# A two-layer kernel on one core: new order at both ends of the first attention, and SiLU from exponentials and logarithms

## The reference, cut to what matters

```python
x = x + xattn(norm(x), ctx)     # 16 heads; head h sees every 16th key, from h on: 128 keys for each
x = x + ssm(norm(x))            # below
x = x + swiglu(norm(x))         # weights of three levels, activations of 8 bits
x = x + gated(norm(x), ctx)
x = x + self_attention(norm(x)) # 16 heads, relative bias
x = x + mlp(norm(x))            # 8 bits

def ssm(x):
    xi, res = split(x @ W_in)                  # 256 channels each
    u = silu(conv4(xi) + conv_b)
    dt, B, C = split(u @ W_x)                  # 8, 16, 16
    delta = softplus(dt @ W_dt + b_dt)
    h = exp(delta * A) * h + delta * B * u     # step by step over 128 tokens, 16 states
    y = sum(h * C) + u * D
    return (y * silu(res)) @ W_out
```

## Time and profile before

| | us |
|---|---|
| median of 3 runs | 279.73 |
| lowest, highest | 277.42, 280.04 |
| span of the profiled execution | 278.8 |
| busy in it: PE, DVE, ACT, POOL | 209.7, 205.7, 151.6, 74.6 |

### The profile page before, as it was taken

How to read it: one execution, slowest core, us unless ns; L and a number is a source line. 1 busy time by engine, 2 the same in 40 slices (tenths; PEclk the granted TensorE clock), 3 DMA queues, 4 the chain that set the end, 5 groups by cost and what they waited for, 6 DMA issues and landing times.

```text
span 278.8 us, 4790 instructions
## 1 busy us (share of the span) xinstructions
PE 209.7 (75%) x1557; PEld 141.2 (51%) x1559; DVE 205.7 (74%) x585; ACT 151.6 (54%) x510; POOL 74.6 (27%) x73
## 2 busy tenths in 40 slices
PE   6896988898786977777762577999996699973313
PEld 4475877676752322222131354777785688851102
DVE  6358648873069999999957975767767499985675
ACT  4357659643685555555317773245336689853420
POOL 5013000049305777777794010000001000001000
PEclk9688999999979799999996899999999899997555
DMA  7999700068830000000000005000000000000001
GB/s 225 429 393 414 317 2 2 0 74 93 94 45 0 1 0 1 0 0 0 2 1 0 1 0 150 2 0 2 0 1 0 4 1 2 0 4 0 4 0 38
DMA packets 6745, 16.06 MB, mean 58 GB/s; under 512 B 320, under 2 KB 5056, under 8 KB 5696
## 3 DMA queue, kind: packets, MB, share of 16 engines
q1 hardware_dynamic: 6720, 15.75, 19.7%
HBM read 13.39 MB, written 2.35 MB: 56 GB/s over the span
## 4 chain that ended last, share of the span: by engine, by line
PE 38%; DVE 24%; POOL 13%; issue 12%; ACT 9%; DMA 2%; POOLq 0%; SPq 0%; another core or an unknown queue 0%; DVEq 0%; ACTq 0%
PE bank L1076 31%; POOL region L392 13%; ACT probs L477 3%; PE bank L1416 3%; DVE region L775 2%; DVE region L758 2%; DMA ctx_T_sb<-ctx_T 2%; PE bank L1189 2%; DVE neg_max L753 1%; DVE xn L685 1%; DVE stats L680 1%; PE bank L1093 1%; DVE ext L1040 1%; DVE ext L1041 1%; DVE v_heads L698 1%
## 5 line engine op out<-in xcount | busy, mean ns | idle before, releaser
L1076 PE MATMUL bank<-region,early_sb 128*128 128x512 f32 x64 | 36.8, 661 | 11.8 <-POOL region L392 11.6
L392 POOL TENSOR_TENSOR region<-region 128x512 f32<-128x512 f32 x32 | 40.5, 1268 | 14.5 <-DVE region L900 14.5
L900 DVE TENSOR_TENSOR_SCAN region<-region,bank 128x512 f32<-128x512 f32 x32 | 38.7, 1211 | 0.0
L1076 PE MATMUL bank<-k_groups,region 128*128 128x128 f32 x256 | 35.7, 285 | 1.2 <-ACT k_groups L459 1.2
L1076 PEld LDWEIGHTS bank<-k_groups,region 128*128 128x128 f32 x256 | 32.2, 198 | 3.2 <-ACT k_groups L459 1.8
L361 POOL TENSOR_TENSOR xb<-x,rows_sb 128x512 f32<-128x512 f32 x3 | 3.8, 1261 | 101.0 <-DVE x L790 43.2
L477 ACT ACTIVATE probs<-bank,neg_max 128x128 f32<-128x128 f32 x64 | 22.6, 367 | 12.9 <-DVE neg_max L753 12.5
L1076 PE MATMUL bank<-ctx_T_sb,region 128*32 128x128 f32 (+1 forms) x288 | 26.8, 345 | 3.4 <-DMA ctx_T_sb<-ctx_T 2.2
L477 ACT ACTIVATE probs<-region,neg_max 128x128 f32<-128x128 f32 x64 | 24.9, 390 | 5.7 <-DVE neg_max L758 5.5
L1076 PEld LDWEIGHTS bank<-region,early_sb 128*128 128x128 f32 x64 | 10.1, 195 | 33.2 <-POOL region L392 32.6
L775 DVE COPY region<-bank 128x512 f32<-128x512 f32 x32 | 21.8, 682 | 5.6 <-PE bank L1189 5.6
(11 more groups left out here) (198 smaller groups left out, 410.1 us busy)
## 6 DMA issues: line engine op xcount, KB each, us to landing
ctx_sb<-ctx SPq DMA_DIRECT2D x4, 1024.0 KB, 24.5
ctx_T_sb<-ctx_T SPq DMA_DIRECT2D x3, 1024.0 KB, 10.5
late_sb<-late SPq DMA_DIRECT2D x1, 2416.0 KB, 18.4
bias_scratch<-bias_vec SPq DMA_DIRECT2D x1, 2040.0 KB, 24.7
ctx_T_sb<-ctx_T SPq DMA_DIRECT2D x2, 512.0 KB, 6.2
region<-bias_scratch SPq DMA_DIRECT2D x1, 1024.0 KB, 5.7
early_sb<-early SPq DMA_DIRECT2D x1, 512.0 KB, 3.7
region<-taps SPq DMA_DIRECT2D x1, 512.0 KB, 18.9
```

Source lines behind the costliest of these rows:

```text
L392: done(pool.tensor_tensor(read[:, k % 3, :], state[:, k % 3, :], c_sb[:, n % 2, :], ALU.mult), "read")
L900: done(dve.tensor_tensor_scan(state[:, k % 3, :], decay[:, k % NDA, :], bank[3 + k % 3][:, :], 0.0, ALU.mult, ALU.add), "state")
L1076: return pe.matmul(dst, lhsT, rhs, start=start, stop=stop)
```

## The change

It has four parts.

The opening: GpSimd clears `v_heads` before the DMAs arrive; layer norm, turn and queries of batch 0 go ahead of the other three; scores wait for the keys of their own head group only (`k_first`); `turn_xn(0, 0, 2)`, `(0, 0, 3)`, the other queries and the first values stand inside the attention's first steps. `keys` and `values` of the later batches move one step later on ScalarE.

The stages: `PROJECT`, `ADD`, `RSTD` and `NORM` come one step earlier, in both attentions, and VectorE scales before it copies the turned probabilities. In ph 0 the loop ends at step 15 (`STEPS`), and the rest is written out.

SiLU: u and the gate are made as z * exp(-log(1 + exp(-z))) with the table that is loaded anyway, in three passes on ScalarE and a product; the gate's passes stand in the state loop (`GATE_STEPS`), its product behind the loop on VectorE.

The way to the loop: columns 0 to 383 (batches 0 to 2) and 384 to 511 (batch 3) have their own products with W_x, splits and step sizes; the fills are gone; one quantisation moves behind the loop.

```diff
-INVERSE, INVERSE_T, VALUES, SCALE, PROJECT, ADD, RSTD, NORM, TURN = 6, 7, 8, 9, 10, 11, 11, 12, 13
+INVERSE, INVERSE_T, VALUES, SCALE, PROJECT, ADD, RSTD, NORM, TURN = 6, 7, 8, 9, 9, 10, 10, 11, 13
+STEPS = 4 * NB, NG * (NB - 1) + NORM + 1
-CHANNELS = {17: [(0, 0)], 18: [(0, 1)], 23: [(0, "gates"), (1, "gates")], 25: [(1, 0), (1, 1)]}
-FILLS = {"early_in": 20, "bc_parts": 16, "hidden": 12, "hidden_rest": 12, "swiglu_out": 4}
+FILLS = {"early_in": 20, "hidden": 12, "hidden_rest": 12, "swiglu_out": 4}
+PIECES = [(0, 2), (2, 3), (3, 4)]
+FIRST = 3 * P
+GATE_STEPS = (6, 8, 10, 12, 14, 16)
...
             done(pool.memset(ones[:, :], 1.0), "ones_set")
             link(pool.memset(wz[:, :, :, :, :, :].rearrange("p i j g k d -> p (i j g k d)"), 0.0))
+            done(pool.memset(v_heads[:, :, :, :, :, :].rearrange("p b j g k d -> p (b j g k d)"), 0.0), "pads")
...
+            def sigmoids(i):
+
+                act.wait_ge(S["xc"], i + 1)
+                link(act.activation(sig[:, :, piece(i)], du[:, :, piece(i)], ACT.Exp, scale=-1.0))
+                link(act.activation(sig[:, :, piece(i)], sig[:, :, piece(i)], ACT.Ln, bias=1.0))
+                done(act.activation(sig[:, :, piece(i)], sig[:, :, piece(i)], ACT.Exp, scale=-1.0), "sig")
...
+            def log_terms(i, hfs, cols):
+
+                act.wait_ge(S["dt_sum"], i + 1)
...
+            copy_xn_T(0, 2)
+            copy_xn_T(0, 3)
+            for hf in range(DH):
+                done(act.activation(skip[:, hf, :], ident, ACT.Copy, scale=C("d_skip", hf)), "skip")
...
+            copy_xn_T(1, 1)
+            heads_out(2)
+            rsqrt_var(1, 2)
+            heads_out(3)
+            rsqrt_var(1, 3)
+            sigmoids(0)
+            sigmoids(1)
+            sigmoids(2)
+            low_rank(0, 3, slice(0, FIRST))
+            log_terms(0, slice(0, 1), slice(0, FIRST))
+            low_rank(1, 4, slice(FIRST, T))
+            log_terms(1, slice(0, DH), slice(FIRST, T))
+            log_terms(2, slice(1, 2), slice(0, FIRST))
...
+            split(0, 3, slice(0, FIRST))
+            biased(0, 1, slice(0, 1), slice(0, FIRST))
+            split(1, 4, slice(FIRST, T))
+            biased(1, 6, slice(0, DH), slice(FIRST, T))
+            stepped(0, slice(0, 1), slice(0, FIRST))
+            dve.wait_ge(S["u"], 2)
+            done(dve.tensor_tensor(du[:, 0, 0:FIRST], delta[:, 0, 0:FIRST], u[:, 0, 0:FIRST], ALU.mult), "du")
+            stepped(1, slice(0, DH), slice(FIRST, T))
...
+            biased(2, 2, slice(1, 2), slice(0, FIRST))
...
+            for hf in range(DH):
+                ins = dve.tensor_tensor(gate[:, hf, :], gate[:, hf, :], gate_s[:, hf, :], ALU.mult)
...
+            turn_probs(4 * NB - 2)
+            turn_xn(1, 1, 1)
+            heads(0, 2)
+            convolve(0, 0)
+            turn_probs(4 * NB - 1)
+            project(0, 2)
+            turn_inverse(0, 3)
+            heads(0, 3)
+            convolve(0, 1, range(2))
+            project(0, 3)
+            convolve(0, 1, range(2, CONV))
+            turn_xn(1, 1, 2)
+            convolve(1, 0)
+            convolve(1, 1)
+            turn_xn(1, 1, 3)
...
+            gates(0, 0, 3, bank[5][:, 0:FIRST])
+            done(gates(1, 0, 3, bank[7][:, 0:FIRST]), "gates_ps")
+            convolve(2, 0)
+            convolve(2, 1)
```

More of the change, by code:

```diff
@@ L205, in two_layers @@
         read = turn("ssm", [3, T])
-        skip = turn("skip", [DH, P], at=loop_at + 12 * T)
+        gate_s = turn("ssm", [DH, T])
+        skip = sb("skip", [P, DH, P])
         y2 = turn("ssm", [DH, T])
@@ L743, in attention @@
                 i_out = 1 if ph == 0 else 5
[L744 removed]
+                for t in range(STEPS[ph]):
                     if t < 4 * NB:
@@ new lines, in clamped, with split @@
+            def clamped(i):
+                dve.wait_ge(S["conv_ps"], DH * (i + 1))
+                if i == 2:
+                    dve.wait_ge(S["gates_ps"], 2)
+                for hf in range(DH):
+                    ins = dve.tensor_scalar(du[:, hf, piece(i)], conv_at(i, hf), C("conv_b", hf), LEAST, ALU.add, ALU.max)
+                done(ins, "xc")
+            def split(i, at, cols):
+                n = cols.stop - cols.start
+                dve.wait_ge(S["bc_hi"], i + 1)
+                for rest, end in ((bank[at][:, 0:n], 2 * BC), (bc_rest[:, cols], BC)):
+                    link(dve.tensor_tensor(bc_rest[0:end, cols], rest[0:end, :], bc_parts[0:end, cols], ALU.subtract))
+                    done(dve.tensor_copy(bc_parts[0:end, cols], bc_rest[0:end, cols]), "bc_parts")
+                    dve.wait_ge(S["bc_parts"], 2 * i + (1 if end > BC else 2))
```

486 lines of the change are left out of this document (275 added, 211 removed).

## The result

The changed kernel takes 292.37 us (median of 4 runs, 292.17 to 297.96), the kernel before 279.88 beside it (277.42 to 280.98). The ratio is 1.050, 95% interval 1.042 to 1.057: slower, above the predicted range of 276.3 to 287.3. The profiled execution's span is 290.1 us, 11.3 more than before.

What follows compares the result with a forecast made beforehand. No engine bounds opening or hand-over, only who waits for whom; VectorE bounds the second attention. 2.4 + 0.4 + 1.4 = 4.2 on the 278.8 span, plus 0.9, gives 283.9 us; range 276.3 to 287.3, own range 281.5 to 286.

Steps and rivals of the forecast that it cites:

- The opening: Start to last neg_max of first attention: first exponential 14.3 instead of 17.39, 3.1 us gained, 1.15 left at 55.5.
- From the last neg_max to low_rank: Convolution and gates behind the first attention: low_rank starts at 75.1 instead of 77.70, 2.6 us earlier.
- The hand-over: From low_rank to the first scan: 12.8 us instead of 7.85, first scan at 87.9; bounds 10.3 and 13.8.
- The loop and its end: State loop: low clock at its start 0 (bounds 0, +2); gate products at its end +0.4 us (0, +1.4).
- The 0.8 that the prediction worked out by the rule: Loop's end: by the SBUF exclusion rule the gate products' term would be about 0.8, the time 284.3.
- Weight quantisation behind the loop: Weight quantisation 2 moved behind the loop, where nothing asks for it for 20 us: costs nothing.
- The second attention: Projection ahead of next scores makes neg_max wait 1.2 and 0.85 us: +1.4, bounds -0.6 and +2.4.
- batch 2 has no scores behind it and wins 0.6: Second attention: batch 2's projection delays no scores, so 0.6 us is won within the +1.4.
- Gain kept: Opening's 3.1 us survive to the last neg_max and the second attention absorbs its wait: 280.6 us; chance 0.27.
- TensorE paced: First attention: TensorE never waits, low_rank starts at 68.9; second attention unharmed: 276.3 us; chance 0.20.
- two holes of four microseconds: First attention: TensorE paced was supported by the old order having two holes of four microseconds.
- Everything bites: Low clock in first loop steps +2, exclusion at loop's end +0.4, second attention +1.0 more: 287.3 us; chance 0.15.

Runs made afterwards that it cites:

- e15_best: Kernel before plus the change's opening, 40 fills behind the state block's output, bias_scratch write behind first scan, 4 swiglu fills for 12: 275.9 us, 0.988.
- e16_place: Changed kernel with PROJECT, ADD, RSTD, NORM one step later in the second attention, scaling still ahead of the copy: 288.1 us, ratio 1.032.
- e7_warm_bias: Changed kernel with 8 TensorE fills after the turn of step 14's probabilities and the bias_scratch write behind the first scan: 288.7 us, ratio 1.035.
- e9_gap: Changed kernel with 48 TensorE fills behind the state block's output product: 291.3 us, ratio 1.036.
- e5_open: Kernel before with the change's opening alone, keys and values of later batches one step later: 276.9 us, ratio 0.988.
- e6_bias: Kernel before with only the write of bias_scratch moved behind the first scan of the state loop: 278.9 us, ratio 1.004.
- e11_open_gap_bias: Kernel before with the change's opening, 40 fills behind the state block's output and the bias_scratch write behind the first scan: 276.3 us, ratio 0.980.
- e1_ph1: Changed kernel with PROJECT, ADD, RSTD, NORM one step later and VectorE's old order, in the second attention only: 289.1 us, ratio 1.032.
- e2_quant: Changed kernel with the third weight quantised ahead of the state loop again: 291.1 us, ratio 1.040.
- e3_warm: Changed kernel with 8 TensorE fills after the turn of the probabilities of step 14: 290.9 us, ratio 1.037.
- e4_merge: Changed kernel with one hand-over for all 512 columns, biased(0) and biased(1) ahead of the split: 288.7 us, ratio 1.032.
- e14_quant_fewer: Changed kernel with the third weight quantised ahead of the loop and 4 fills instead of 12 in the swiglu block: 290.1 us, ratio 1.038.
- e13_fewer: Changed kernel with 4 fills instead of 12 (hidden_rest) in the swiglu block: 292.0 us, ratio 1.046.

## Why the prediction was wrong

**The opening: right, with luck.** First exponential 14.27 (forecast 14.3), last neg_max 55.21 (55.5). The gain of 3.1 shrinks to 1.44 as the schedule said, and by the wait that it named: the scores of step 12 wait 1.51 us for their keys, until 44.98 (forecast 45.3). In the other kernels with this opening the first exponential came between 12.39 (e15_best) and 14.38 (e16_place), and in the eleven that share the changed kernel's whole first attention the last neg_max came between 53.51 (e7_warm_bias) and 56.25 (e9_gap). So to hit both within 0.3 us was luck. And one term came true without its reason: the products from 9 to 12.8 took twice as long, as forecast, but the row of the granted clock says 1.00 there (last section).

**From the last neg_max to low_rank: the step that failed.** "conv(0,0) until 61.25" and "Low_rank starts at 75.1". It started at 77.63. That step took every duration at full clock, for before the clock was 1.00 from 57 to 65; a lower clock was no term of the sum there. The new order leaves TensorE less dense from 55 on (busy 0.98 of the 2.00 us from 55 to 57, 2.00 before), and the clock fell, to 0.61 and 0.54: heads(2) 1.70 for 1.08, eight passes 3.78 for 1.86, the turn 1.06 for 0.60, 3.0 in all by these rows. With the clock at 1.00 (e7_warm_bias) the stretch took 19.27, 3.15 less than the 22.42, and the forecast was 19.6: the schedule was right, its clock was not. A second slip lies in what the step was measured against: the 21.05 of before had a hole of 1.84 in it. Measured without it (19.05 in e5_open, e6_bias, e11_open_gap_bias and e15_best), the rewritten way to low_rank wins nothing even at full clock, so the 1.45 us that the step forecast as won are no more than what the hole cost before.

**The hand-over: right.** 12.80 us, forecast 12.8, within 0.01 in e1_ph1, e2_quant, e3_warm and e7_warm_bias too. The rounds begin where they were forecast: 3.61, 7.64 and 10.43 us behind low_rank's start, for 3.58, 7.55 and 10.4. And e4_merge shows that the cut, with the order that goes with it, is its cause.

**The loop and its end: undersized.** At its start TensorE was at 0.50 and the skip products took 3.56 us for 1.88; the buffers cover nearly all (0.30, bounds 0 and +2). At the end I took +0.4 where the two products took 2.54 us for 1.38 and GpSimd's reads 2.93 for 2.48; the stretch grew by 0.90. The +0.4 was a middle taken without a row. By the Trainium skill, "SBUF — State Buffer", section "SBUF: two separate sides", a VectorE instruction with two SBUF inputs and a GpSimd instruction that reads SBUF exclude each other for a whole instruction. The trace agrees: the last read (145.1 to 146.8) and the second product (145.6 to 147.4) took 1.71 us for 1.27 and 1.75 for 0.69, and that product ended 0.55 us behind the read. The 0.8 that the prediction worked out by the rule was nearer than what it took.

**Weight quantisation behind the loop: a cost taken for nothing.** "Where nothing asks for it for 20 us" looked at who waits for the weight, not at what runs beside it while it is made. GpSimd is busy 4.74 of the 5.00 us from 153 to 158, and of VectorE's small steps there q_mul takes 0.56 for 0.17 and q_up 0.67 for 0.22: 0.84 us, settled by e2_quant. The other 1.3 of this stretch go with a lower clock (0.84 and 0.75 for 1.00 from 163 to 173), but may be the luck of one profile.

**The second attention: mechanism right, size off.** The waits are where the prediction put them: neg_max 0.87 for batch 0 (forecast 1.2), 1.3 in two waits for batch 1 (0.85). Together 2.2 for 2.05, so these terms were right. The term that was mis-sized is the last: "batch 2 has no scores behind it and wins 0.6" did not come; in its place VectorE waits another 0.24 for turned probabilities and 0.63 for o_T behind 259. ScalarE's exponentials wait too (1.13 at the first); that these waits are what delays the end is argued, not shown. +3.14 for +1.4, over the bound of +2.4; e16_place gives 3.8 back by the step of the four stages alone.

**The rivals.** Gain kept and TensorE paced fell: first exponential to last neg_max took 40.9 us, not less than the 39.3 of before. The "two holes of four microseconds" that spoke for TensorE paced are not in the trace of before: TensorE's longest wait for another engine from 17 to 57 us is 1.7, and all of them together are 6.1. Everything bites had three of the right places, but put the low clock at the loop's start alone. Two sums slip: 51.0 and 17.7 are 68.7 and not 68.9, and with both lower bounds the forecast's own range begins at 279.4 and not 281.5. Neither changes the outcome.

## What to carry to other kernels

A schedule by hand needs the clock of each stretch as an input: where a new order leaves TensorE thinner, price what comes next at the lower level, as the upper bound at least; here, with 3.0 us, that was the largest missing term. An early piece that shares one queue with its late pieces saves little (1.1 us here), and the two extra rounds between ScalarE and VectorE cost 4.4 us. Look for a wait that nothing explains in the kernel you start from: the change gets the credit for it. And a stretch of one profiled execution can be 1 to 2 us off the next one's; read it in several kernels that share it before you explain it. When work moves to a "free" engine, look at what the other engines do in the same microseconds, and not only at who needs the result.

## What the runs showed of the hardware that was not expected

TensorE can stand for 1.84 or 3.25 us with no semaphore that it waits for (kernel before, e3_warm). In the thirteen kernels in which a write kept the DMA engines 0.84 busy, no 16 KB instruction packet of q8 ran from 50 to 67 us; in the five without it one ran at 55.4 to 59.5. Both holes end 1.2 to 1.4 us after the late packet's end.

The clock's fall is not a property of a place: the same wait of 1.02 us was followed by 0.61 in the changed kernel and by 1.00 in e14_quant_fewer, and what helped in one stretch (more fills in e9_gap, fewer in e13_fewer) was followed by a fall in a later one. What sets it stays open.

In the opening of the changed kernel the scores of step 0 took 2.07 us, twice their 1.06, and the keys ahead of them 1.94 for the 1.08 of later ones, with the granted clock at 1.00 in that stretch; DMA moved 431 GB/s then. Either the clock's row is wrong there or something else halves TensorE's speed. No run here tells which.
